# A sandwich of attention and quantised projection: queries turned before they are split, a smaller correction step, and a new issue order

## The reference

```python
h = layernorm(layernorm(x)) * ln_w + ln_b
q, k, v = heads(h @ w_q), heads(h @ w_k), heads(h @ w_v)     # 16 heads of 16
q, k = rope(q, theta), rope(k, theta)
s = einsum('bhkd,bhqd->bhkq', q, k) * 0.25                   # 'k' indexes q's rows
t = 1 + s + 0.5 * s * s                                      # Taylor softmax
att = (t / t.sum(-1)) @ v
x = x + layernorm(att @ w_o)
xq = quantise(layernorm(x), blocks of 32, FP6 grid)          # and the weight too
x = x + layernorm(xq @ w.T + bias)
```

## Time and profile before

| what | value |
|---|---|
| median of 3 runs | 692.29 us |
| the profiled execution, own time | 691.8 us |
| its span, first to last instruction | 690.0 us |
| PE busy | 662.7 us (96%) |
| DVE busy | 572.7 us (83%) |
| ACT busy | 559.2 us (81%) |
| POOL busy | 370.2 us (54%) |
| granted TensorE clock, mean | 1.000 |

### The profile page before, as it was taken

How to read it: one execution, slowest core, us unless ns; L and a number is a source line. 1 busy time by engine, 2 the same in 40 slices (tenths; PEclk the granted TensorE clock), 3 DMA queues, 4 the chain that set the end, 5 groups by cost and what they waited for, 6 DMA issues and landing times.

```text
span 690.0 us, 19674 instructions
## 1 busy us (share of the span) xinstructions
PE 662.7 (96%) x6444; PEld 504.7 (73%) x6444; DVE 572.7 (83%) x1443; ACT 559.2 (81%) x1546; POOL 370.2 (54%) x724
## 2 busy tenths in 40 slices
PE   5889999999999999999999999999999999999787
PEld 4776667787778777777787778777777877766576
DVE  6999998888888888898879888888888888884575
ACT  3468879888898989888888988889898888978753
POOL 3655445556545565565555556564655565553344
DMA  6200000202011020201111020101102010010101
GB/s 201 62 3 31 2 32 2 78 16 71 17 48 47 14 73 18 77 10 47 48 39 48 17 77 18 54 33 48 42 15 78 17 41 17 18 47 17 47 31 39
DMA packets 28706, 28.31 MB, mean 41 GB/s; under 512 B 2368, under 2 KB 28480, under 8 KB 28608
## 3 DMA queue, kind: packets, MB, share of 16 engines
q1 hardware_dynamic: 27792, 26.27, 11.6%
q10 hardware_dynamic: 816, 0.79, 0.3%
HBM read 18.66 MB, written 8.39 MB: 39 GB/s over the span
## 4 chain that ended last, share of the span: by engine, by line
PE 89%; ACT 4%; issue 3%; DVE 2%; POOL 1%; DMA 1%; SPq 0%; ACTq 0%; POOLq 0%; DVEq 0%
PE ps_mt L686 11%; PE ps_f L527 11%; PE ps_o L578 9%; PE ps_o L581 8%; PE ps_qk L483 4%; PE ps_qk L486 4%; PE ps_qk L484 4%; PE ps_tr L483 4%; PE ps_w L483 4%; PE ps_tr L550 4%; PE ps_w L486 4%; PE ps_w L484 4%; PE ps_o L615 3%; PE ps_tr L486 2%; PE ps_tr L484 2%
## 5 line engine op out<-in xcount | busy, mean ns | idle before, releaser
L789 ACT ACTIVATE feat<-ps_f 128x512 f32<-128x512 f32 x256 | 153.7, 603 | 4.0 <-PE ps_f L527 3.6
L527 PE MATMUL ps_f<-qT,selr 128*128 128x512 f32 x320 | 134.0, 426 | 4.5 <-ACT feat L791 4.5
L414 DVE TENSOR_TENSOR kf<-kf 128x1024 f32<-128x1024 f32 (+1 forms) x128 | 137.8, 1117 | 0.3
L1329 POOL TENSOR_TENSOR ve_y<-var_y,epst 128x1 f32<-128x1 f32 x64 | 44.9, 702 | 155.2 <-ACT squares_y L893 155.2
L686 PEld LDWEIGHTS ps_mt<-kf,vp 128*32 128x32 f32 x2048 | 65.9, 110 | 45.9 <-issue 42.9
L686 PE MATMUL ps_mt<-kf,vp 128*32 128x161 f32 x2048 | 82.2, 301 | 3.6 <-issue 1.3
L852 ACT ACTIVATE vp<-ps_tr 128x256 f32<-128x256 f32 x64 | 24.6, 384 | 61.2 <-PE ps_tr L486 59.7
L836 ACT ACTIVATE hT<-ps_tr,lnb,lnwx 128x128 f32<-128x128 f32 x128 | 51.6, 453 | 23.2 <-PE ps_tr L563 22.8
L1329 POOL TENSOR_TENSOR ve_f<-var_f,epst 128x1 f32<-128x1 f32 x64 | 16.7, 262 | 98.6 <-ACT squares_f L912 98.6
L578 PE MATMUL ps_o<-feat,main 128*32 128x512 f32 x512 | 67.8, 602 | 0.0
L581 PE MATMUL ps_o<-feat,rm 128*32 128x512 f32 x512 | 66.7, 592 | 0.0
(11 more groups left out here) (196 smaller groups left out, 2022.3 us busy)
## 6 DMA issues: line engine op xcount, KB each, us to landing
xc<-L_attn_x SPq DMA_DIRECT2D x16, 512.0 KB, 4.0
result<-fin SPq DMA_DIRECT2D x64, 128.0 KB, 1.7
xa<-L_attn_x SPq DMA_DIRECT2D x15, 512.0 KB, 4.1
wkqv<-L_attn_w_kv ACTq DMA_DIRECT2D x2, 256.0 KB, 4.3
xa<-L_attn_x SPq DMA_DIRECT2D x1, 384.0 KB, 5.1
csel<-shape_constants SPq DMA_DIRECT2D x1, 320.0 KB, 5.4
wkqv<-L_attn_w_q ACTq DMA_DIRECT2D x1, 256.0 KB, 4.6
wf<-L_ffn_weight SPq DMA_DIRECT2D x1, 256.0 KB, 5.2
```

Of the source, the lines that this page charges most:

```text
L414: return eng.tensor_tensor(dims(row, F_MAIN, [[FW, heads], [HD, NR], [1, HD]]), dims(row, F_LIN, [[FW, heads], [0, NR], [1, HD]]), dims(ro ...
L527: pe.matmul(ps_f[i % 2][:, :], selr[:, i], qT[:, par, quad], start=True, stop=True).then_inc(sel_done, 1)
L789: act.activation(feat[:, p2, i], ps_f[i % 2][:, :], ACT.Square).then_inc(squared, 1)
L1329: pool.tensor_tensor(ve[c][:, t.two:t.two + 1], variance, floor, ALU.add).then_inc(pool_step[c], 1)
```

## The change

It has five parts.

1. **Queries.** `rope_add` writes keys only. `add_q` (DVE) writes the rotated queries unsplit to qf. `turn_q` turns qf with two float32 transposes, one for two quads. `high_q` (ACT, two instructions of 64 partitions) copies the high part from ps_tr to qT, and `low_q` (DVE, two of 64 partitions, each writing the other half of the partitions) subtracts. `copy_q`, the old `high_q`, POOL's `low_q`, qsp and the float32r identity go. ps_tr is now free after DVE's `low_q` (qT_split).
2. **Correction.** `turn_sums` turns the pair products only. `rest_terms` (DVE, two instructions a sequence) combines squares and single features into rest. `rest_matrix` puts these into the correction's bank with 16 float32 products of 32 columns instead of four of 128. restT and crest go.
3. **Load.** theta is loaded first, and the small constants in two transfers (64 columns, then the identity).
4. **A piece moved between engines.** `low_v`, a set-up subtraction of 512 columns, moves from DVE to POOL.
5. **Order.** All lags, the order in each engine's `step`, FIRST and FINAL are new. t1 and t2 now get their own waits, since sin runs a step ahead of cos.

```diff
+            def quads(turned, rows, t, odd):
+                return dims(turned[rows, t.par, odd, t.tile * P:t.tile * P + 1], 0, [[2 * T, 2], [1, P]])
...
+            sp.dma_start(th[:], theta.to_broadcast([P, 1])).then_inc(theta_in, 16)
             sp.dma_start(xa[:, 0, 0:1], x_seq[0][:, 0:1]).then_inc(x0_in, 16)
-            sp.dma_start(th[:], theta.to_broadcast([P, 1])).then_inc(theta_in, 16)
-            sp.dma_start(small[:], const[:, 0:NSMALL]).then_inc(ident_in, 16)
+            sp.dma_start(small[:, P:NSMALL], const[:, P:NSMALL]).then_inc(cols_in, 16)
+            sp.dma_start(ident, const[:, 0:P]).then_inc(ident_in, 16)
...
-                pe.wait_ge(qlo_ready, t.n)
+                pe.wait_ge(q_ready, t.n)
...
-                for qd in range(NQ):
-                    mm = pe.matmul(ps_tr[:, qd * P:(qd + 1) * P], qsp[:, t.two, qd].rearrange("p a b -> p (a b)"), identr[:, :],
-                                   start=True, stop=True)
+                for pair in range(2):
+                    mm = pe.transpose(ps_tr[:, pair * P:(pair + 1) * P], qf[:, t.two, pair * P:(pair + 1) * P], ident)
...
                 for qd in range(NQ):
-                    pe.transpose(ps_mt[0][:, qd * P:(qd + 1) * P], mts[:, qd, F_MAIN:F_SQ], ident)
-                for qd in range(NQ):
-                    mm = pe.transpose(ps_mt[1][0:2 * HD, qd * P:(qd + 1) * P], mts[:, qd, F_SQ:NF], ident)
+                    mm = pe.transpose(ps_mt[0][:, qd * P:(qd + 1) * P], mts[:, qd, F_MAIN:F_SQ], ident)
...
-                for h in range(HQ):
-                    mm = pe.matmul(ps_mt[0][VW * h:VW * (h + 1), 0:P], crest, restT[:, :, VW * h:VW * (h + 1)],
-                                   start=False, stop=True, skip_group_check=True)
+                for qd in range(NQ):
+                    for h in range(HQ):
+                        mm = pe.matmul(ps_mt[0][VW * h:VW * (h + 1), VW * qd:VW * (qd + 1)], rest[:, qd], ident[:, VW * h:VW * (h + 1)],
+                                       start=False, stop=True, skip_group_check=True)
...
-                act.activation(restT[0:2 * HD].rearrange("p a b -> p (a b)"), ps_mt[1][0:2 * HD, :], ACT.Copy).then_inc(mm_copied, 1)
...
+                for odd in range(2):
+                    rows = slice(64 * odd, 64 * odd + 64)
+                    ins = act.activation(quads(qT, rows, t, odd), ps_tr[rows, 0:2 * P].rearrange("p (a b) -> p a b", a=2), ACT.Copy)
+                ins.then_inc(qT_high, 1)
...
-                dve.tensor_tensor(dims(kf[:, t.two, 0, 0:1], F_LIN, [[F_Q - F_LIN, 2], [FW, H], [1, HD]]),
-                                  t1[:].rearrange("p (a h d) -> p a h d", a=2, d=HD),
-                                  t2[:].rearrange("p (a h d) -> p a h d", a=2, d=HD), ALU.add).then_inc(rope_ready, 1)
+                dve.tensor_tensor(kf[:, t.two, :, F_LIN:F_EXT], t1[:, 0:D].rearrange("p (h d) -> p h d", d=HD),
+                                  t2[:, 0:D].rearrange("p (h d) -> p h d", d=HD), ALU.add).then_inc(rope_ready, 1)
+            def add_q(t):
+                dve.wait_ge(qk_read, 2 * t.n)
+                wait(dve, qT_done, t.n - 2)
+                dve.tensor_tensor(qf[:, t.two], t1[:, D:2 * D], t2[:, D:2 * D], ALU.add).then_inc(q_ready, 1)
+            def low_q(t):
+                dve.wait_ge(qT_high, t.n)
+                for odd in range(2):
+                    rows, other = slice(64 * odd, 64 * odd + 64), slice(64 - 64 * odd, 128 - 64 * odd)
+                    ins = dve.tensor_tensor(quads(qT, other, t, odd), ps_tr[rows, 0:2 * P].rearrange("p (a b) -> p a b", a=2),
+                                            quads(qT, rows, t, odd).bitcast(F32), ALU.subtract)
+                ins.then_inc(qT_split, 1)
...
+            def rest_terms(t):
+                dve.wait_ge(mt_copied, t.seq + 1)
+                wait(dve, ps_done, t.seq)
+                dve.tensor_scalar(rest[:, :, HD:VW], mts[:, :, F_LIN:NF], ALPHA / 2, None, ALU.mult).then_inc(lins_scaled, 1)
+                dve.wait_ge(lins_scaled, t.seq + 1)
+                dve.scalar_tensor_tensor(rest[:, :, 0:HD], mts[:, :, F_SQ:F_LIN], ALPHA**2 / 2, rest[:, :, HD:VW],
+                                         ALU.mult, ALU.subtract).then_inc(rest_ready, 1)
...
 FINAL = {
+    "project_out": (1, 1, 1, 1, 1, 1, 1, 1, 1, 1, 1, 1), "turn_ffn_input": (1, 1, 1, 1, 1, 1, 1, 1, 1, 2, 4, 5),
```

More of the change, by code:

```diff
@@ L55 @@
 NF = F_EXT
-F_Q = F_EXT + NR
-FW = F_Q + HD
+FW = F_EXT + NR
 VW = 2 * HD
@@ L84 @@
-    "scale_ln": 0, "rstd_y": 13, "low_h": 1, "add_s": 14, "add_x": 0, "rstd_s": 14, "low_q": 3, "rstd_x": 0,
-    "add_f": 15, "rstd_f": 15, "products_2": 2, "tables": 1, "add_y": 12,
+    "turn_z": 0, "warm_up": 0, "select_1": 6, "project_out": 12, "turn_ffn_weight": 11, "select_2": 6,
+    "turn_ffn_input": 14, "rest_matrix": 3, "fill_a": 2, "attend": 7, "sum_features": 2, "turn_q": 2, "select_3": 6,
+    "ffn": 14, "fill_b": 2, "drain_b": 16, "turn_attention": 11, "turn_sums": 2, "select_4": 6, "project_kq": 0,
@@ L502, in warm_up @@
             def warm_up():
-                idle_products(ps_o, 12)
+                idle_products(ps_o, 10)
             def fill():
@@ L731, in step @@
                 each(n, "project_kq", project_kq)
+                each(n, "project_v", project_v)
+                late(n, "drain_a", drain)
+                each(n, "select_0", select, 0)
                 each(n, "turn_quads", turn_quads)
-                each(n, "turn_z", turn_z)
-                late(n, "drain_b", drain)
-                each(n, "select_0", select, 0)
-                each(n, "project_out", project_out)
             every_step(step)
@@ L798, in copy_sums @@
                 wait(act, cb_ready, s)
+                wait(act, rest_ready, s)
                 for half in range(2):
@@ new lines, in step @@
+                each(n, "inverse_scales", inverse_scales)
+                each(n, "to_grid", to_grid)
+                each(n, "rope_cos", rope_cos)
+                setup(n, "weight_candidate_low", weight_candidate_low)
+                each(n, "from_grid", from_grid)
+                setup(n, "weight_distances", weight_distances)
+                each(n, "rope_add", rope_add)
+                once(n, "rest_terms", rest_terms)
+                setup(n, "angles", angles)
+                each(n, "extend_k", extend_k)
@@ new lines, in step @@
+                setup(n, "split_bias", split_bias)
+                setup(n, "weight_choice", weight_choice)
+                each(n, "low_q", low_q)
+                once(n, "constant", constant)
+                setup(n, "low_ffn_weight", low_ffn_weight)
+                each(n, "low_attention", low_attention)
+                each(n, "normalise_x", normalise_x)
+                setup(n, "centre_wo", centre_wo)
+                setup(n, "weight_result", weight_result)
+                setup(n, "low_wo", low_wo)
```

262 lines of the change are left out of this document (115 added, 147 removed).

## The result

The changed kernel takes 707.37 us (median of 4 runs, 705.79 to 707.83) against 692.31 of the kernel before beside it: ratio 1.0215, 95% interval 1.0197 to 1.0232. It is 15 us slower; 684 was predicted, and 671 to 696 as the range. The profiled span grew from 690.0 to 705.6.

A forecast was written before the change was run, and what follows sets the result against it. PE was taken to bound the middle, DVE the first part, PE and ACT's chain the end. Span 690.0 - 4.9 (first part's +4.2 included) - 3 = 682.1, with the offset to the run time 684 us; range 671 to 696.

The forecast's parts named there:

- DVE becomes the bound: Rival, middle: wait for the denominators stays 0.84, a tile takes 10.08 us, 702 us in all; chance 0.18.
- the sum for DVE: DVE's work in the middle: 8.43 us a tile plus 0.71 and 0.1 becomes 9.24, hidden behind PE's 9.73.
- the prediction's own rule: Middle: DVE stays hidden while its waits are below 0.49 us a tile; from 0.67 on DVE's bound costs time.
- The middle: 51 tiles from the thirteenth z to PE's last turning: 9.73 instead of 9.91 us each, ending at 594.6 against 599.5.
- the first part: Up to DVE's thirteenth z, DVE-bound: 8.5 + 1.2 - 1.5 - 4 = +4.2 us, the thirteenth z at 98.4.
- the end: Behind PE's turning of the last tile: 3 us off 90.5, bounds 6.7 off and as much on.
- PE's sum: PE in the middle: 0.88 + 0.35 - 0.63 + 0.14 = 0.74 us less a sequence, 0.18 a tile.
- the queries: PE: two float32 transposes instead of four products of the split queries, 0.22 us less a tile.
- the sums' turning: PE turns only the first half of the sums: 0.46 instead of 0.81 us, 0.35 less a sequence.
- the small products: PE, correction's second half: 16 products of 32 columns take 0.85 us instead of 0.22, 0.63 more a sequence (0 to 1.06).
- The products: DVE's pair of products in the first part loses POOL's interference, 0.49 us in eleven tiles: 4 us taken of 5.4.
- The start: First part: low_v leaves DVE and frequencies fill its wait for the first tile; first rotation 1.5 us sooner (0 to 2.5).

The follow-up runs named there:

- Experiments 1 and 2: 1: changed kernel, ACT's copy_rest behind FFN input's high part, 696.23 us; 2: low_q cut to 4 of 128 columns, on changed kernel 698.30, on 1 694.90.
- Experiment 4: Changed kernel, x before theta: 706.40 us; frequencies later too: 707.26; both with copy_rest and scale_ln later: 694.85; 12 idle products added: 693.54.

## Why the prediction was wrong

**The rival named "DVE becomes the bound" came, and by a smaller wait than it asked for.** The step that failed is the sum for DVE: 9.24 us a tile, 0.49 below PE's 9.73, so that DVE hides behind PE. The runs show 9.61 of work, with PE at 9.67 when nothing holds it up: 0.06 of slack. Then a wait came that the prediction did not have. It looked only at the waits of the kernel before; it noted that the copy of rm now stands ahead of the FFN input's high part, counted that for PE (half of 0.28 us a sequence), and did not ask who waits behind it on ACT. DVE does, 1.2 us a sequence, 0.29 a tile. By the prediction's own rule this wait alone would have been hidden (9.24 + 0.29 = 9.53); with 9.61 it gives 9.90, the tile that was measured. Experiments 1 and 2 show both halves: without the wait a sequence is 0.99 shorter, and with DVE's work at 9.23, the size that had been forecast, the wait costs 0.35.

The middle holds 12 of the 23 us by which the forecast was missed (9 less forecast, 2.7 more measured), the first part 6.6, the end 5.2.

**What DVE's sum had too small.** 0.81 us were added to a tile, 9.24 in all; 1.13 were measured, 9.61. A plain step of the changed kernel:

```profile
300.35 0.42 DVE L1129 TENSOR_TENSOR kf<-t 128x256 f32<-128x256 f32 x1
300.80 0.23 DVE L1149 COPY kf<-kf 128x128 f32<-128x128 f32 x1
301.06 0.86 DVE L1142 TENSOR_TENSOR qT<-ps_tr,qT 64x256 fp32r<-64x256 f32 x2
301.95 0.42 DVE L1191 TENSOR_TENSOR attT_l<-ps_o,attT_h 128x256 fp32r<-128x256 f32 x1
302.29 0.41 DVE L1098 TENSOR_SCALAR z<-xa,mv,rs_x 128x256 f32<-128x256 f32 x1
```

0.23 of the difference is `low_q`: 0.89 a pair (301.06 to 301.95) and not 0.66. Half the partitions cost no less: attT_l, with as many columns on all 128, lasts the same 0.42. But the row behind attT_l starts 0.34 after it, and each half of `low_q` holds DVE for 0.44; the 0.33 taken was such an overlapping step. Why the halves do not overlap, no run separates. The rest is mostly rows behind which the next one waits: the addition of the keys holds DVE for 0.45 here (0.33 forecast), its extension, now right behind it, for 0.26 instead of 0.13, the inverse of the scales for 0.20 instead of 0.09. And z, which in some steps now runs beside POOL's share of the products, lasts 0.66 there instead of 0.41. Against it y lost POOL's interference (641 to 426 ns in the mean).

**PE's sum was right to 0.05 a tile, though not each of its terms.** With the wait gone a tile is 9.67 against 9.90, 0.23 less where 0.18 was forecast: the queries 0.19 a tile (0.22), the sums' turning 0.45 a sequence (0.35), the small products 0.22 more (0.63), rm 0.07 less (0.14). That makes 1.06 a sequence, of which PE's other rows took 0.14 back. The small products had been taken near the count of instructions; they cost 0.43, about twice what their columns alone would.

The Trainium skill, "TensorE: Matmul & The Clock Gate" (section "Wait — 56ns, not 53.3ns?"), gives about 25 ns as the least distance of two starts; 32 of them in 0.43 us are 13 ns each, so this floor does not hold here. The page "TensorEngine Tiling (Array Packing)" of the Trainium skill (section "Key Properties") says that different tiles of the array can work in parallel; that agrees, since the four heads' products go to four groups of 32 output partitions. No run here changes the groups, so that they are the reason is not shown.

**One slip of bookkeeping.** 9.91 a tile ran from DVE's thirteenth z to PE's turning of the last tile, which is 3.7 us behind its z; from z to z it was 9.835. That moved 3.7 us between middle and end and did not change the sum.

**The first part: right in kind, too low.** Predicted +4.2, measured +10.8. The products gave back 3.5 (4 predicted). DVE's other work grew by 11.7 and not 9.7, `low_q` alone by 8.9. The start, predicted 1.5 sooner, was 3.0 later: theta first was taken as harmless, and the frequencies as filling a wait. Experiment 4 shows three gates in series (x0 6.45, the constants 7.58, the layer norm's vectors about 8), each of which hides the next, and a fourth, the clock.

By the rule that the prediction took from the page "SBUF — State Buffer" of the Trainium skill (section "Who interferes with whom"), the products would get all of their 0.49 back and `low_q` would not be slowed. The trace agrees on both. Ten pairs stand in this stretch, not eleven; the eight that took 2.57 beside POOL's product take 0.95 and 1.22 now, with POOL's share through before DVE's begins, and the ten give back 3.5 of the 5.4. `low_q` holds DVE for 0.89 a pair at the first tiles and in the middle alike, with POOL's product beside it or without.

**The end.** 3 us less predicted, 2.2 more measured. The steps got shorter as expected (6.92 instead of 7.09), and what follows the last att took it back (22.7 against 16.1); that is the step that failed here, and its cause stays open.
